# Toeplitz operand with falling rows from sixteen DRAM copies of the taps, without a reversed copy of x

## What is computed

```python
# block 0: a long convolution per head h, masked by length
u_m = u * mask                                   # mask: position < length[b]
K   = 2 * einsum('hn,hnl->hl', Cs, exp(P)).real  # 32 heads x 512 taps, from 64 modes
y   = irfft(rfft(u_m, 2L) * rfft(K, 2L))[:L]     # causal convolution with K
x   = x + (y + u_m * D) * mask
# block 1: a gated MLP (512 -> 1376 -> 512) with LoRA tables picked per batch element
gate, up = x @ Wg.T + lora, x @ Wu.T + lora
x   = x + ((silu(gate) * up) @ Wd.T + lora)
```

## Time and profile before

| what | value |
|---|---|
| median of the runs | 558.69 us (558.26 to 558.87) |
| the profiled execution's own time | 559.0 us |
| its span, first to last instruction | 557.3 us |
| TensorE busy | 519.2 us (93%) |
| VectorE, ScalarE, GpSimd busy | 256.3, 200.5, 39.8 us |
| DMA: bytes, mean rate | 53.19 MB, 95 GB/s |
| mean granted TensorE clock | 0.995 |

### The profile page before, as it was taken

One profiled execution on the slowest core, in us unless ns is written; L12 is line 12 of the kernel. 1 busy time (PEld: TensorE's weight loads), 2 busy tenths in 40 slices (PEclk: granted clock), 3 DMA queues, 4 the chain that ended last, 5 costly groups with the idle time before them and its releaser, 6 DMA issues.

```text
span 557.3 us, 10115 instructions
## 1 busy us (share of the span) xinstructions
PE 519.2 (93%) x3169; PEld 472.5 (85%) x3169; DVE 256.3 (46%) x556; ACT 200.5 (36%) x427; POOL 39.8 (7%) x55
## 2 busy tenths in 40 slices
PE   0097899999999999999999999999999999999997
PEld 0097787989898989999898989898989898999986
DVE  7873267544444434353435353534444443435341
ACT  6790008333333433242323233323333343324221
POOL 1006700100000000000000000000000000000000
PEclk9999899999999999999999999999999999999999
DMA  7899991312030404030304031211203040404000
GB/s 275 284 339 390 319 315 48 73 56 69 28 99 9 115 0 120 4 111 13 111 13 107 16 93 31 84 39 54 69 25 98 8 116 0 120 3 111 13 21 19
DMA packets 32306, 53.19 MB, mean 95 GB/s; under 512 B 7586, under 2 KB 16194, under 8 KB 32290
## 3 DMA queue, kind: packets, MB, share of 16 engines
q1 hardware_dynamic: 32290, 53.00, 31.9%
HBM read 48.69 MB, written 4.28 MB: 95 GB/s over the span
## 4 chain that ended last, share of the span: by engine, by line
PE 86%; DVE 5%; DMA 5%; ACT 1%; issue 1%; SPq 0%; DVEq 0%
PE ps_g L982 21%; PE ps_u L982 20%; PE ps_db L1020 13%; PE ps_da L1020 13%; PE ps_x L1011 3%; PE ps_x L962 3%; PE ps_g L936 2%; DMA toep<-kpad 2%; DMA kpad<-k_sb 2%; PE ps_u L936 2%; PE ps_g L992 2%; PE ps_u L992 2%; PE ps_g L993 2%; PE ps_u L993 2%; PE ps_x L1054 1%
## 5 line engine op out<-in xcount | busy, mean ns | idle before, releaser
L475 ACT CAST b_spl<-b_raw 64x512 fp32r<-64x512 f32 (+1 forms) x96 | 54.6, 570 | 98.6 <-PE ps_u L993 79.3
L800 DVE TENSOR_TENSOR b_spl<-b_raw,b_spl 64x512 fp32r<-64x512 f32 (+1 forms) x96 | 60.4, 630 | 53.8 <-ACT b_spl L475 50.1
L982 PE MATMUL ps_g<-w_hi,x_hi 128*128 128x512 f32 (+1 forms) x192 | 72.7, 379 | 1.4 <-DVE x_lo L894 1.4
L982 PE MATMUL ps_u<-w_hi,x_hi 128*128 128x512 f32 (+1 forms) x192 | 71.4, 372 | 0.0
L982 PE MATMUL ps_u<-w_lo,x_hi 128*128 128x512 f32 (+1 forms) x192 | 71.3, 371 | 0.0
L982 PE MATMUL ps_u<-w_hi,x_lo 128*128 128x512 f32 (+1 forms) x192 | 71.3, 371 | 0.0
L982 PE MATMUL ps_g<-w_lo,x_hi 128*128 128x512 f32 (+1 forms) x192 | 71.1, 370 | 0.0
L982 PE MATMUL ps_g<-w_hi,x_lo 128*128 128x512 f32 (+1 forms) x192 | 71.0, 370 | 0.0
L836 DVE TENSOR_TENSOR h_act<-h_act,ps_u 128x512 f32<-128x512 f32 (+1 forms) x48 | 30.4, 633 | 54.1 <-PE ps_u L993 54.0
L1020 PE MATMUL ps_da<-wd_hi,ht_hi 128*128 128x288 f32 (+1 forms) x176 | 54.6, 310 | 0.0
L1020 PE MATMUL ps_db<-wd_hi,ht_hi 128*128 128x288 f32 (+1 forms) x176 | 53.3, 303 | 0.0
(11 more groups left out here) (167 smaller groups left out, 917.8 us busy)
## 6 DMA issues: line engine op xcount, KB each, us to landing
a_raw<-atab SPq DMA_DIRECT2D x64, 152.0 KB, 2.5
toep<-kpad SPq DMA_DIRECT2D x16, 512.0 KB, 7.7
b_raw<-btab SPq DMA_DIRECT2D x128, 64.0 KB, 2.1
um<-xr SPq DMA_DIRECT2D x16, 256.0 KB, 5.3
x<-xT SPq DMA_DIRECT2D x8, 512.0 KB, 6.8
w_raw<-wgu SPq DMA_DIRECT2D x8, 512.0 KB, 9.2
out<-y_sb SPq DMA_DIRECT2D x15, 256.0 KB, 2.1
b_raw<-btab SPq DMA_DIRECT2D x64, 44.0 KB, 1.8
```

The lines of the kernel that those rows point to most:

```text
L475: nc.scalar.copy(b_spl[0:LR, up, 0:w], b_raw[slot][:, up * w:(up + 1) * w]).then_inc(b_hi, 1)
L800: V.tensor_tensor(b_spl[LR:P, up, 0:w], b_raw[slot][:, up * w:(up + 1) * w], b_spl[0:LR, up, 0:w].bitcast(F32), ALU.subtract).then_inc(b_l ...
L982: T.matmul(ps[:, 0:w], xs[:, q, kb, :], ws[:, kb, col:col + w], start=(kb == 0 and xs is x_hi and ws is w_hi), stop=False)
```

## The change

A second DRAM tensor `kcopy` holds the padded taps sixteen times. After a group's taps are stored, SP waits for them and copies the group's eight heads from `kpad` to all sixteen copies with one DMA (sixteen rows of 8 x 640 floats, 320 KB, the source repeated with a step of 0). The Toeplitz operand is then read from the copies, one DMA of 256 KB per head: sixteen outer rows, each from its own copy, of eight rows whose start falls by one element. Row p now starts at element 128 - p and belongs to input position p. So `xr`, `um`, `load_um` and their semaphores go, and the matmuls read `x` itself; the convolution waits for its group of x in place of um. The order on SP is written anew: all of x with pieces 0 to 3 ahead of the first store, pieces 4 to 7 around the second, pieces 8 to 11 between the Toeplitz loads of pairs 4 to 7, and a copy behind each store. The copy and every Toeplitz load wait on semaphores of the step before (`k_out`, `k_copied`).

```diff
-def program(nc, xT, xr, wgu, wd, atab, btab, prm, lens, idx, out):
+def program(nc, xT, wgu, wd, atab, btab, prm, lens, idx, out):
...
+        kcopy = nc.dram_tensor("kcopy", (NCOPY, NH, P + NL), F32, kind="Internal")
...
-            um = sb(pa, "um", [P, RC, 2 * KB * NB])
...
-        def shifted_taps(pair):
-
-            return bass.AP(tensor=kpad, offset=pair * (2 * (P + NL)) + 1, ap=[[1, P], [P + NL, 2], [1, NL]])
+        def group_rows(tensor, g, dims):
+
+            return bass.AP(tensor=tensor, offset=g * HG * (P + NL), ap=dims)
+
+        def falling_taps(head):
+
+            rows = P // NCOPY
+            return bass.AP(tensor=kcopy, offset=head * (P + NL) + P,
+                           ap=[[NH * (P + NL) - rows, NCOPY], [-1, rows], [1, NL]])
...
+            def copy_taps(g):
+                sp.wait_ge(k_out[g], 16)
+                sp.dma_start(group_rows(kcopy, g, [[NH * (P + NL), NCOPY], [1, HG * (P + NL)]]),
+                             group_rows(kpad, g, [[0, NCOPY], [1, HG * (P + NL)]])).then_inc(k_copied[g], 16)
+
             def load_toep(pair, slot, group):
 
-                sp.wait_ge(k_out[group], 16)
+                sp.wait_ge(k_copied[group], 16)
                 wait(sp, conv_ps, pair - RC + 1)
-                sp.dma_start(toep[:, slot, :, :], shifted_taps(pair)).then_inc(toep_in[slot], 16)
-
-            def load_um(pair, slot, first):
-                if not first:
-                    sp.wait_ge(conv_ps, pair - RC + 1)
-                sp.dma_start(um[:, slot, :], xr[bass.ds(pair * P, P), :]).then_inc(um_in[slot], 16)
+                for h in range(2):
+                    sp.dma_start(toep[:, slot, h, :], falling_taps(2 * pair + h)).then_inc(toep_in[slot], 16)
...
-            for pair in range(RC):
-                load_um(pair, pair, True)
-            load_x(0, 0)
-            load_x(0, 1)
-            for n in range(2 * KB):
-                load_piece(n)
+            for g in range(NG):
+                load_x(g, 0)
+                load_x(g, 1)
+                if g < KB:
+                    load_piece(g)
             sp.wait_ge(idx_in, 16)
             ids0 = indices(0, 0)
             sp.wait_ge(zero_out, 16)
             store_taps(0)
-            load_piece(2 * KB)
+            copy_taps(0)
             for pair in range(RC):
                 load_toep(pair, pair, 0)
-            for n in range(2 * KB + 1, NP_GU):
+            for n in range(KB, 2 * KB - 1):
                 load_piece(n)
-            load_x(1, 0)
             store_taps(1)
-            load_x(1, 1)
-            load_x(2, 0)
+            load_piece(2 * KB - 1)
+            copy_taps(1)
             for pair in range(RC, 2 * RC):
-                load_um(pair, pair - RC, False)
                 load_toep(pair, pair - RC, 1)
-                if pair == RC:
-                    load_x(2, 1)
+                load_piece(KB + pair)
                 if pair >= RC + 2:
                     store_taps(pair - RC)
-                    load_x(3, pair - RC - 2)
+                if pair >= RC + 3:
+                    copy_taps(pair - RC - 1)
+            copy_taps(NG - 1)
...
             for pair in range(2 * RC, PAIRS):
-                load_um(pair, pair % RC, False)
                 load_toep(pair, pair % RC, pair // RC)
...
-                pe.wait_ge(toep_in[slot], 16 * (pair // RC) + 16)
-                pe.wait_ge(um_in[slot], 16 * (pair // RC) + 16)
+                pe.wait_ge(toep_in[slot], 32 * (pair // RC) + 32)
+                pe.wait_ge(x_in[2 * pair // HG], 32)
...
-                        v = um[:, slot, h * KB * NB:h * KB * NB + (KB - d) * NB]
+                        v = x[:, 2 * pair + h, 0:KB - d, :].rearrange("p k b -> p (k b)")
```

More of the change, by code:

```diff
@@ L26 @@
 FB = -(-NF // P)
+NCOPY = 16
 FLAST = NF - (FB - 1) * P
@@ L161, in program @@
         toep_in = [sem(f"toep_in{i}") for i in range(RC)]
-        um_in = [sem(f"um_in{i}") for i in range(RC)]
+        k_copied = [sem(f"k_copied{g}") for g in range(NG)]
         conv_ps, x1_ok = sem("conv_ps"), sem("x1_ok")
@@ L1101 @@
     xT = np.asarray(x).reshape(NB, NH, KB, P).transpose(3, 1, 2, 0).reshape(P, NH * KB * NB)
-    xr = xT.reshape(P, NH // 2, 2 * KB * NB)[::-1].transpose(1, 0, 2).reshape(NH // 2 * P, 2 * KB * NB)
     def interleave(g, u):
@@ L1129 @@
     prm = np.concatenate([half, half], axis=0)
-    arrays = {"xT": xT, "xr": xr, "wgu": wgu, "wd": wd, "atab": atab, "btab": btab, "prm": prm,
+    arrays = {"xT": xT, "wgu": wgu, "wd": wd, "atab": atab, "btab": btab, "prm": prm,
               "lens": np.asarray(itok_B_8_3872), "idx": np.asarray(itok_B_2_6)}
```

## The result

The changed kernel takes 569.32 us (median of 4, 568.59 to 569.71), the kernel before 558.78 in the same job: a ratio of 1.0184, 95% interval 1.0168 to 1.0199. It is 10.5 us **slower**, where 3 us faster was forecast, and lies above the forecast's range of 551.5 to 561.0. One execution of a later run (split rows, no copies) took 662.45 us at a granted clock of 0.764, and that run's median leaves it out.

A forecast was written before the change was run, and what follows sets the result against it. DMA was taken to set the pace up to 60.59 us, then TensorE. The last convolution ending at 76.2 against 79.16 wins 3.0 us: 559.0 - 3.0 = 556.0, with the runs' median 0.3 lower, 555.7 us; range 551.5 to 561.0.

The forecast's parts named there:

- The mechanism of the gain: Before the MLP, 16 um loads (4 MiB, some 10.8 us of queue) go; they delay what is queued behind them.
- the sum: Chain of stores, copies, loads and convolutions by group; last convolution ends at 76.2 us against 79.16, 3.0 us won.
- The row rate: Toeplitz loads from the copies in a running queue move at 390 GB/s, the packets having the same length.
- The copies' price: Four copies inside DRAM, 2.8 us each to landing; copies 0, 1 and 2 lie on the path.
- Shortest landings: A Toeplitz load with nothing queued ahead lands in 3.9 us for 512 KB, the shortest of the 16.
- the second store 1.5: Group 1's store of taps, issued at 35.0, lands at 36.5 us, with the 1.5 of group 0.
- near 48: Group 2's store of taps, in the queue behind pair 6 and piece 10, lands near 48 us.
- SP's issues: On SP, 32 Toeplitz loads replace 16 um and 16 Toeplitz loads: no difference.
- Rival 2: Serial copies at 3.8 us each take all that was won: 558.7 us, 17% for within 0.2%.
- rival 1: Falling rows are slower: every Toeplitz load at 203 GB/s, last convolution near 86, 566 us; 15%.
- The clock: If the 2.4 us gap ahead of convolution 8 sets the clock back, the wait for pair 10 covers it, else 0.5.

The follow-up runs named there:

- the square: Four runs of the changed kernel's loads: plain rows without copies 555.5 us, with copies 564.8; split rows without copies 560.8, with copies 569.3 (the change).
- eights (246): Kernel before, with um, x and weight pieces 0 to 11 read as sixteen outer rows of eight: 581.04 us, ratio 1.0400; 246 GB/s from 10 to 20 us.
- fours (381): Kernel before, with um, x and weight pieces 0 to 11 read as thirty-two outer rows of four: 558.75 us, ratio 1.0008; 381 GB/s.

## Why the prediction was wrong

**The mechanism of the gain was right.** um's loads delay what stands behind them; without them 4.4 us are won in the timed runs, and the work behind the convolutions is unchanged. The loss came from what takes their place, and from what the sum took for the waits. The last convolution ended at 89.2, where the sum had 76.2. Of these 13.0 us the split makes 5.2, the copies 2.1 more than the sum gave them, and 5.7 were missing before either came in.

**The row rate failed (5.2 us).** The step that took 390 GB/s in a running queue "because the packets have the same length" is wrong: 259 to 265 GB/s. I had the two ends, 203 and 383, and a rival for the lower at 15%, priced at 566 us with its turning point at about 280 GB/s. The rate lies below that point, and the slow rows explain half of the loss against the kernel before: 4.6 to 5.2 us in the square. Of what that rival named, the falling step and the distance between the copies played no part (265 GB/s with rising rows, 285 against 290 from one copy); the split did. The Trainium skill (DMA: Bandwidth & Descriptors, The descriptor swizzle) says that a transfer over 128 partitions is dealt out in groups of four neighbours, each engine writing one port of SBUF. By that rule eight neighbours per engine would put two engines on a port; the runs with eights (246) and fours (381) agree with it, but no run here shows which engine writes which partition, so the port itself stays an explanation. I hadn't weighed that rule.

**The copies' price failed (2.1 us).** I took 2.8 us a copy; they took 3.46, 4.03 and 3.39 on the chain. By the sum's own terms without copies, the load of pair 0 lands at 26.0 and the last convolution ends at 26.0 + 14.4 + 28.9 = 69.3, so the sum of 76.2 gave the copies 6.9 us; with plain rows they cost 9.0. The change would then have lost 4.9 at the yardstick even with the row rate I assumed. The Trainium skill's rate for copies between HBM tensors (DMA: Bandwidth & Descriptors, Latency and other measured facts), 214 GB/s, which I had set beside the sum and not in it, pointed the right way: 3.5 us each, an estimate.

**Shortest landings were taken for usual ones (most of the 5.7 us).** With plain rows and no copies the last convolution ended at 75.0 (70.20 + 4.83), not at 69.3. The sum gave every first load of a group 3.9 us, the least of sixteen, and the second store 1.5, the landing with an empty queue. In that run group 2's store took 7.48 us, behind the loads, and convolution 9 waited 2.33 us for its operand; some 2 us more are convolution 1 at half speed. In the changed kernel the loads of pairs 0 and 4 landed 4.6 and 4.9 us after the first issue of the pair, the one ahead of convolution 8 about 5.5; group 1's store took 4.04, group 2's 7.23. Group 2's store was to land "near 48"; it landed at 57.87. Slow rows don't explain its 7.23 us: it took 5.96 with plain rows behind the copies, 7.48 with plain rows and no copies, and 8.86 in the kernel before, which stood in the earlier trace rows ahead of the forecast.

**SP's issues** were costed as no difference; a split load takes 0.59 us to issue against 0.38, and fours, which keep that time, stay 1.7 us above plain rows.

**The rivals.** Rival 2 (copies eat what was won, at 3.8 us each) had the copies' price about right and the row rate wrong; rival 1 the other way round. Each was priced alone, and the case that holds both, which is what happened, stood nowhere. Added to the forecast, their prices (3.0 and 10.3 us) give 569.0. That this is the measured time is luck: rival 1 gave slow rows some 10 us where they cost 5, and that made up for the landings, which no rival had; rival 2's own case, plain rows behind the copies, took 564.8 and not 558.7.

**The clock** played the part that was said: the gap ahead of convolution 8, 4.68 in place of 2.4 us, set it back, to a granted 0.58 from 66.9 to 71.0 us, and 4.28 us came of it. Convolution 1 at half speed (4.50 us) was not in the sum; in the changed kernel the wait for pair 4's load covered it.

## What to carry to other kernels

A load whose source is cut into sixteen outer rows of eight is another transfer than one of 128 rows, though packets, bytes and engine count are the same: keep 128 plain outer rows, or fours, and try the pattern on one load before building on it. A round trip through DRAM that is added between a producer and its load should be priced at landings under traffic, not at the shortest one (here 3.0 to 4.0 us for 320 KB, and 2.3 to 9.4 for a store of 16 KB on a queue in use), and once per time it stands on the chain. Where two unknown costs belong to one change, price the case that has both.

## What the hardware showed that was not expected

The outer shape of a DMA's source alone changed the rate from 404 to 246 GB/s at the same share of busy engines, and thirty-two by four brought it to 381. In the traces a 4 KB packet of these loads takes 159 ns in the median plain and in fours, and 267 in eights. A load whose 128 source rows are split over two dimensions took SP about 0.2 us more per issue (0.59 against 0.38 to 0.43), in eights and fours alike. The number of dimensions isn't it: the Toeplitz load of the kernel before has three in its source too, the third for its two heads, and took 0.38. A small store issued by GpSimd on its own queue landed after 3.1 to 5.9 us while SP's queue was in use, where the same stores on SP's queue took 2.3 to 9.4: the late ones sooner, the early one later, and the kernel was no faster for it. What keeps such a store for 3 us and more on a queue of its own was not tried.
